# An adaLN block with a Mamba-2 scan: sections in four column groups, the second softplus chain in pieces, and a last stage that projects two tiles ahead

## What is computed

```python
mod = (silu(c) @ wmod).reshape(4, 6, 1, 512)          # sa, ca, ga, sb, cb, gb
ga = sign(ga) * max(|ga|, 0.25); gb likewise
h = layernorm(x) * (1 + ca) + sa
xBCzA = h @ in_proj_w.T                               # 1024 x, 512 B, 512 C, 1024 z, 64 A_log
xBC = silu(conv1d(xBC, 4 taps) + bias)
dt = softplus(A_log)
y = ssd_chunk_scan(x, -dt, B, C) + D * x / dt         # 64 heads of 16, 8 groups, state 64
x = x + ga * ((y * silu(z + z_bias)) @ out_proj_w.T)
h = layernorm(x) * (1 + cb) + sb
x = x + gb * (h @ binarize(w_ffn).T + b_ffn)
```

## Time and profile before

| | |
|---|---|
| median of 3 runs | 722.79 us (719.93 to 724.25) |
| the execution that was profiled | 725.2 us, span in the trace 723.5 us |
| busy, share of the span | PE 91%, DVE 71%, ACT 52%, POOL 52% |
| first stage | to 103.2 us |
| main loop | 103.2 to 583 us |
| last stage | from 583 us |

### The profile page before, as it was taken

How to read it: one execution, slowest core, us unless ns; L and a number is a source line. 1 busy time by engine, 2 the same in 40 slices (tenths; PEclk the granted TensorE clock), 3 DMA queues, 4 the chain that set the end, 5 groups by cost and what they waited for, 6 DMA issues and landing times. The chain is left out here.

```text
span 723.5 us, 21285 instructions
## 1 busy us (share of the span) xinstructions
PE 660.5 (91%) x8347; PEld 497.3 (69%) x8347; DVE 516.7 (71%) x913; ACT 379.1 (52%) x818; POOL 374.9 (52%) x464
## 2 busy tenths in 40 slices
PE   5559797989999999999999999999997999999994
PEld 2244455767777777777777777777775767778783
DVE  3569739796787777777778677777788567676663
ACT  1573633545654545564644564556665545555552
POOL 7544401244653634555445365464556757777771
PEclk9678899999999999999999999999999999999995
DMA  9354211133312121132123143321213755333401
GB/s 265 79 205 121 72 31 54 62 94 106 95 63 93 60 71 65 59 129 67 34 84 104 37 137 107 111 94 49 92 68 101 224 156 153 117 117 117 132 30 43
DMA packets 61915, 70.53 MB, mean 97 GB/s; under 512 B 13972, under 2 KB 33460, under 8 KB 61816
## 3 DMA queue, kind: packets, MB, share of 16 engines
q1 hardware_dynamic: 56376, 69.12, 29.6%
q10 hardware_dynamic: 5440, 0.05, 0.4%
HBM read 54.45 MB, written 14.70 MB: 96 GB/s over the span
## 5 line engine op out<-in xcount | busy, mean ns | idle before, releaser
L1393 DVE SCALAR_TENSOR_TENSOR m_cv<-bank,gpc,m_cv 128x511 f32<-128x511 f32 (+2 forms) x192 | 143.3, 747 | 31.9 <-ACT m_cv L1304 27.3
L1149 PE MATMUL bank<-h_hi,w_hi 128*128 128x512 f32 x384 | 161.0, 419 | 4.8 <-ACT p_hf L647 1.7
L1149 PE MATMUL bank<-h_hi,w_lo 128*128 128x512 f32 x384 | 153.9, 401 | 0.0
L1149 PE MATMUL bank<-h_lo,w_hi 128*128 128x512 f32 x384 | 153.4, 400 | 0.0
L1528 POOL TENSOR_TENSOR m_S<-m_S,m_cd 128x128 f32<-128x128 f32 x96 | 39.7, 413 | 159.3 <-DVE m_S L1453 80.2
L1304 ACT ACTIVATE m_cv<-bank,gpc 128x512 f32<-128x512 f32 x96 | 71.8, 748 | 76.5 <-PE bank L1149 76.5
L1149 PEld LDWEIGHTS bank<-h_hi,w_hi 128*128 128x128 f32 x384 | 74.4, 194 | 20.7 <-issue 6.8
L1149 PEld LDWEIGHTS bank<-h_hi,w_lo 128*128 128x128 f32 x384 | 73.8, 192 | 17.3
L1518 POOL TENSOR_TENSOR m_Xw<-m_Xp,wend 128x256 f32<-128x256 f32 x64 | 39.8, 621 | 87.8 <-ACT m_Xp L1324 87.8
L1149 PEld LDWEIGHTS bank<-h_lo,w_hi 128*128 128x128 f32 x384 | 74.4, 194 | 14.1
L1316 ACT ACTIVATE m_M<-bank 128x512 f32<-128x512 f32 x128 | 76.2, 595 | 12.4 <-PE bank L1158 10.4
(11 more groups left out here) (172 smaller groups left out, 1283.8 us busy)
## 6 DMA issues: line engine op xcount, KB each, us to landing
m_ea<-ea_scratch SPq DMA_DIRECT2D x32, 256.0 KB
m_dd<-dd_scratch SPq DMA_DIRECT2D x32, 256.0 KB
y_scratch<-m_t SPq DMA_DIRECT2D x16, 512.0 KB, 3.3
h_lo_place<-y_scratch SPq DMA_DIRECT2D x16, 512.0 KB, 4.3
p_wm<-in_L_wmod_dram SPq DMA_DIRECT2D x6, 1024.0 KB, 8.1
m_wraw<-in_L_attn_in_proj_w_dram SPq DMA_DIRECT2D x18, 256.0 KB, 3.1
p_xt<-in_L_attn_input__dram SPq DMA_DIRECT2D x16, 256.0 KB, 5.2
w_lo_place<-in_L_attn_input__dram SPq DMA_DIRECT2D x16, 256.0 KB, 4.5
```

The lines of the kernel that those rows point to most:

```text
L1149: ins = pe.matmul(A[k % 3][:, :], w[:, t, kc, :], h[:, n % NB, kc, :], start=(m == 0), stop=(m == 11))
L1393: ins = dve.scalar_tensor_tensor(out=cv[:, k % 3, lag:], in0=A[k % 3][:, 0:L - lag], scalar=s.gpc[:, gp, o:o + 1], in1=cv[:, k % 3, lag:], ...
```

## The change

On PE, `scT` is widened to 32 columns, all but 4 of them zero. `section(n)` now writes product k into partitions 32k to 32k+31 of the bank, with no accumulation, and `turn_section` multiplies the 128 copied rows with `pick`, a 128x4 matrix of ones and zeros, which turns and adds the four parts. The sections 2 to 5 are later in PE's order, and the normalizations 12 to 15 are on POOL. The loads of the sections 0 and 1 come first, x gets eight places instead of four, and the statistics have a place for every tile, which removes waits. `softplus(1)` and `finish_times(1)` are moved from the end of the first stage into the main loop, and `skips(0)` behind the gates:

```diff
             if n == 2:
-                pe.wait_ge(w_act, 8)
-            if n == 4:
-                pe.wait_ge(h_act, 16)
+                pe.wait_ge(h_act, 15)
+                pe.wait_ge(w_act, 12)
+            if n >= 4:
+                pe.wait_ge(sec_cp, n - 1)
             for k in range(KC):
-                ins = pe.matmul(row_bank(n)[0:NB, :], scT[:, k, :], wm[:, n % 2, k, :], start=(k == 0), stop=(k == KC - 1))
+                ins = pe.matmul(row_bank(n)[32 * k:32 * k + 32, :], scT[:, k, :], wm_of(n)[:, k, :], start=True, stop=True)
...
-                ins = pe.transpose(mod_bank(n)[:, k * NB:(k + 1) * NB], row_of(n)[:, k * P:(k + 1) * P], s.ident[0:NB, 0:NB])
+                ins = pe.matmul(mod_bank(n)[:, k * NB:(k + 1) * NB], row_of(n)[:, k * P:(k + 1) * P], pick[:, :], start=True, stop=True)
...
                     if (v, sl) == (-1, 3):
+                        start.softplus(dve, 1)
+                    if (v, sl) == (0, 3):
+                        start.finish_times(dve, 1)
+                    if (v, sl) == (1, 3):
                         start.sums(dve, 1)
-                    if (v, sl) == (1, 3):
+                    if (v, sl) == (2, 3):
                         start.low_sums(dve, 1)
-                    if (v, sl) == (3, 3):
+                    if (v, sl) == (4, 3):
                         start.skips(dve, 1)
```

`store_decays(1)` and `decays(1)` move one unit later with them. DVE and POOL at the start of the first stage, cut:

```diff
 # DVE
         statistics(dve, 0)
-        for i in range(3):
-            statistics(dve, i + 1)
+        statistics(dve, 1)
+        dve.wait_ge(wa_act, 1)
+        dve.tensor_tensor(wa_lo[:, :, 64:128], s.bank[5][:, 0:KC * NH].rearrange("p (k h) -> p k h", k=KC),
+                          wa_hi[:, :, 64:128].bitcast(F32), ALU.subtract).then_inc(wa_dve, 1)
+        for i in range(6):
             normalize(i)
+            if i == 2:
+                modulation(0)
+                modulation(1)
+            statistics(dve, i + 2)
...
+        for i in range(12, 16):
+            statistics(dve, i)
         softplus(dve, 0)
         finish_times(dve, 0)
         sums(dve, 0)
-        skips(dve, 0)
         low_sums(dve, 0)
 # POOL
         constant_fills()
-        for i in range(4):
+        constant_shapes()
+        for i in range(5):
             root(i)
...
+        for i in range(12, 16):
+            normalize(i)
```

In the last stage, project and y are further ahead, POOL keeps one of its three small operations, and the last tile is handled in four pieces:

```diff
 # PE
-            if not is_last(st) and st.n(1, 1) >= 2:
+            if st.n(1, 2) < NB * TT:
                 for part in range(4):
-                    project(pe, st.n(1, 1), part)
+                    project(pe, st.n(1, 2), part)
             turn(st)
             if not is_first(st):
                 linear(st.prev())
 # ACT
         def step(st):
-            normalize(st)
-            if two_more(st):
-                act.wait_ge(ylo_done, st.n(1, 1))
-                high_y(act, st.next().next())
+            if st.n(1, 1) < NB * TT - 1:
+                normalize(st.next())
+            if four_more(st):
+                high_y(act, ahead(st, 4))
...
+            if is_last(st):
+
+                for k in range(KC):
+                    modulated(st, k, h_hi).then_inc(hhi_done, 1)
+                    modulated(st, k, hf).then_inc(hf_done, 1)
+                return
...
+            if is_last(st.next()):
+                normalize(LAST)
 # POOL
-            pool.tensor_tensor(rstd[:, st.b % 2, 0:1], mv[:, st.b % 2, 1:2], eps[:, :], ALU.add).then_inc(eps_done, 1)
...
-            pool.tensor_scalar(rstd[:, st.b % 2, 2:3], mv[:, st.b % 2, 0:1], rstd[:, st.b % 2, 1:2], -1.0,
-                               ALU.mult, ALU.mult).then_inc(rs_done, 1)
-            if two_more(st):
-                low_y(pool, st.next().next())
+            if four_more(st):
+                low_y(pool, ahead(st, 4))
 # DVE
+        dve.tensor_scalar(rstd[:, st.b % 2, 0:1], mv[:, st.b % 2, 1:2], EPS, None, ALU.add).then_inc(eps_done, 1)
+        dve.tensor_scalar(down[:, st.b % 2:st.b % 2 + 1], mv[:, st.b % 2, 0:1], -1.0, None, ALU.mult).then_inc(eps_done, 1)
```

More of the change, by code:

```diff
@@ L422, in gpsimd @@
             weights(n)
-        root(10)
-        root(11)
+        for i in range(8, 16):
+            root(i)
+        weights(4)
+        weights(5)
+        for i in range(12, 16):
+            normalize(i)
+        weights(6)
+        weights(7)
+        pool.wait_ge(a_v[0], A_END)
         low_part(8)
         low_part(10)
-        for n in range(4, 8):
-            weights(n)
-        for i in range(12, 16):
-            root(i)
         low_part(12)
@@ L538, in vector @@
         low_part(13)
+        convolve(2)
         low_part(15)
-        convolve(2)
         silu(1)
@@ L547, in vector @@
         gates()
[L548 to L549 removed]
+        skips(dve, 0)
     def chained(dve, pb, count):
@@ L687, in scalar @@
         softplus_inputs(0)
+        make_h(8)
+        make_h(9)
+        weights(4)
+        weights(5)
+        make_h(10)
+        make_h(11)
+        linear(0)
+        weights(6)
+        weights(7)
+        linear(1)
+        decays(act, 0)
+        linear(2)
+        tanh(0)
+        make_h(12)
+        make_h(13)
+        tanh(1)
+        make_h(14)
+        make_h(15)
         for n in range(8, 12):
-            make_h(n)
-        for n in range(4, 8):
             weights(n)
-        linear(0)
-        decays(act, 0)
         copy_row(2)
         copy_row(3)
-        linear(1)
-        for n in range(12, 16):
-            make_h(n)
-        linear(2)
-        tanh(0)
-        for n in range(8, 12):
-            weights(n)
-        tanh(1)
         linear(3)
@@ L794, in weights @@
             ins.then_inc(wt_pe, 1)
-        pe.wait_ge(sct_ready, 1)
+        pe.wait_ge(cond_step, 4)
+        section(0)
+        section(1)
         pe.wait_ge(d_wa, 16)
         for k in range(KC):
-            ins = pe.transpose(DTB[:, k * NH:(k + 1) * NH], wa_raw[:, k * P:(k + 1) * P], s.ident[0:NH, 0:NH])
+            ins = pe.transpose(s.bank[5][:, k * NH:(k + 1) * NH], wa_raw[:, k * P:(k + 1) * P], s.ident[0:NH, 0:NH])
         ins.then_inc(wa_pe, 1)
-        turn(0)
-        turn(1)
-        section(0)
-        turn(2)
-        turn(3)
-        section(1)
+        pe.wait_ge(sec_cp, 2)
         turn_section(0)
         turn_section(1)
-        for i in range(4, 8):
+        for i in range(8):
             turn(i)
@@ L812, in tensor @@
             weights(n)
-        pe.wait_ge(wa_dve, 1)
         dt_inputs(0)
-        pe.wait_ge(w_act, 4)
         for i in range(8, 12):
             turn(i)
-        for n in range(4, 8):
-            weights(n)
+        weights(4)
+        weights(5)
         project(0, 0)
         project(0, 1)
+        project(1, 0)
+        project(1, 1)
+        weights(6)
+        weights(7)
+        project(2, 0)
+        project(2, 1)
+        for i in range(12, 16):
+            turn(i)
+        for n in range(8, 12):
+            weights(n)
         section(2)
         section(3)
-        project(1, 0)
-        project(1, 1)
+        project(3, 0)
+        project(3, 1)
         turn_section(2)
         turn_section(3)
-        for i in range(12, 16):
-            turn(i)
-        project(2, 0)
-        project(2, 1)
-        for n in range(8, 12):
-            weights(n)
-        project(3, 0)
-        project(3, 1)
         section(4)
         section(5)
-        pe.wait_ge(w_act, 12)
         end_turn(pe, 0)
+        pe.wait_ge(h_act, 16)
+        dt_inputs(1)
         turn_section(4)
         turn_section(5)
-        dt_inputs(1)
         pe.wait_ge(gate_v, 3)
@@ L1682, in step @@
                 main.store_last(sp)
-            else:
-                store(st.prev())
+            if two_back(st):
+                store(ahead(st, -2))
         run(step)
+        store(ahead(LAST, -1))
         store(LAST)
@@ L1717, in step @@
                 act.wait_ge(main.t1_done, 2 * STEPS)
+            wait(act, hlo_done, st.n(1, -1))
+            if is_last(st):
+                for k in range(KC):
+                    modulated(st, k, h_hi).then_inc(hhi_done, 1)
+                    modulated(st, k, hf).then_inc(hf_done, 1)
+                return
             for k in range(KC):
[L1719 to L1720 removed]
+                ins = modulated(st, k, h_hi)
             ins.then_inc(hhi_done, 1)
[L1722 removed]
             for k in range(KC):
[L1725 to L1726 removed]
+                ins = modulated(st, k, hf)
             ins.then_inc(hf_done, 1)
+            if is_last(st.next()):
+                normalize(LAST)
+        high_y(act, ahead(FIRST, 2))
+        normalize(FIRST)
+        high_y(act, ahead(FIRST, 3))
         run(step)
```

295 lines of the change are left out of this document (159 added, 136 removed).

## The result

The changed kernel takes **716.55 us** (median of 8 runs, 714.72 to 717.99), the kernel before 724.39 on the same chip (8 runs, 719.93 to 725.7). The ratio is 0.9903, 95% interval 0.9877 to 0.9929: faster by about 1%, 7.0 us by the ratio and 7.8 by the medians. Of 23 executions of the kernel before in the first group of experiments, fifteen took 720.1 to 724.0 us and eight took 725.1 to 726.7, so a median of few executions depends on the mix. I had forecast 706.7 and a range of 700.5 to 714.0. So the sign is right, the gain is somewhat less than half of the 16.1 us forecast, and the result lies outside the range. The profiled execution took 717.52 us, with a span of 715.5, which is 8.0 less than the 723.5 of before; the forecast was 16.1 less.

A forecast was written before the change was run, and what follows sets the result against it. PE was taken to bound the kernel, busy 660.5 of 723.5 us, with idle time mainly in the first and last stages. 722.8 - 3 (first stage) - 13.1 (last stage) = 706.7 us; range 700.5 to 714.

The forecast's parts named there:

- rival 5: Last stage: its 5.9 us aren't gained, ACT's wait for project(n+2) replacing its wait for POOL; 712.6 us, chance 0.09.
- rival 1: End of the last stage: the clock falls in the last gap, 3.4 us more, 710.1 us; chance 0.23.
- rival 2: First stage: the sections don't overlap, sections 2 to 5 cost 14.1 instead of 5.2 us; 715.6 us, chance 0.07.
- the row on the diagonal: Main-loop diagonal product: 3.4 us of columns done in 0.86, fourfold overlap; basis for 0.9 us a section.
- rival 6: First stage: POOL's normalizations hold up the first chain, stretching its other half by 2.7 us; 709.4 us, chance 0.06.
- the sum for the first stage: First stage into main loop: loop begins at 98.9, not 103.24; 4.3 us shrink to about -3, bounds -8 and +1.
- The walk through DVE: Main loop: following DVE's order with present durations, m_Ct's second-batch silu ends at 130.8 instead of 134.4.
- rival 4: Turns -1 to 4: chain pieces stop PE and halve its clock; 17 us lost cancel the gain, 25 give 731; chance 0.03.
- Rival 3: Main loop: pieces go under DVE's slack, PE gains 4.3 + 4.6 instead of 3 us; 701 us, chance 0.12.
- The gain of the last stage: Last stage: -5.9 from waits inside, -0.2 at the start, -4.7 and -2.3 at the end; -13.1 us.
- its bound for the first stage, +1: First stage: upper bound of the -3 us sum, if each chain piece stops PE once.

The follow-up runs named there:

- e4: The change with each section again four accumulated 4-row matmuls, turned by 4-row transposes, in the new order; 725.53 us, ratio 1.0024 to the kernel before.
- e5: The change with normalizations 12 to 15 back on DVE behind the first chain; 716.60 us, ratio 0.9922 to the kernel before.
- e2: The change with the last stage of the kernel before, so the new first stage alone; 726.76 us, ratio 1.0053 to the kernel before.
- e6: The change with x tiles 0 to 3 normalized and turned before the section rows are turned; 713.49 us, ratio 0.9878 to the kernel before.
- e3: The change with the second softplus chain in one piece and the first reciprocal back in their old places; 716.96 us, ratio 0.9910 to the kernel before.
- e11: The kernel before with the new last stage, turns 13 and 14 inside the last projection, and the first reciprocal moved into DVE's idle time; 710.90 us, ratio 0.9824.
- e10: The change with x turned first, second chain begun behind the gates, first reciprocal in DVE's idle time, turns 13 and 14 inside the last projection; 711.01 us, ratio 0.9827.
- e9: The change itself measured once more, nothing altered, against the kernel before; 716.47 us, ratio 0.9905.
- e7: The change with the first reciprocal in DVE's idle time after 83 and the second chain begun right behind the gates; 715.63 us, ratio 0.9902.

## Why the prediction was wrong, and where it was right

**Right.** PE alone bounds the last stage, and the period is 7.90 us (rival 5 falls). The clock stays at full speed across the last gaps of 1.43 and 0.97 us (rival 1 falls; it wasn't tried what a gap of 2.3 in one piece does, so that this came out right is in part luck: the gap was split by a wait that I hadn't foreseen). The sections overlap, at 0.96 us each (1.92 for the pair 4 and 5) against 3.60 in e4, where I had 0.9 (rival 2 falls). The estimate from the Trainium skill (TensorE: Matmul & The Clock Gate, Measured speedup vs the span model) was 1.1 to 1.5 us; the measurement decides for the row on the diagonal. POOL's normalizations hold up the chain by less than 1 us and the loop not at all (rival 6 falls, by e5), though each takes two to four times what I gave it. The rule of the Trainium skill (SBUF — State Buffer, Who interferes with whom) agrees with the trace in direction, 0.89 us a step beside POOL's work against 0.72 without; for the chain it changes nothing here, since POOL has other work in that time in either kernel. It costs something behind the chain, where I had not looked for it: the 2.88 us for DVE's two subtractions.

**The step that failed: the sum for the first stage, "-3".** The trace has +1.6 at project 2 (+1.0 at the ninth product), and e2 has +4.3 us on the whole. Nearly all of it was there when the loop began: at 98.9 in the forecast and at 104.14 in the trace, 5.2 us later. My own points of time show where it came from:

- *The start, 2.7 us.* h of tile row 0 begins at 28.18, not at 26. I had looked at which loads and which DVE work stood ahead of the first h, and had left out PE's own order: the turns of the section rows, 3.57 us, and behind them the transposes of x, which in the kernel before were done while ACT was issuing loads. At the end of the first dt_inputs it is 2.9 us (50.95, not 48.0), at the beginning of the chain 3.2 (54.75, not 51.6), and at the end of its sums 2.7 are left. e6 undoes just this and gets 2.5 us back.
- *Between the sums and the last weights on ACT, 2.0 us.* ACT is done with w_act 12 at 84.4, not 79.8, so 4.6 late. ACT waits for the convolution, which stands behind DVE's two subtractions for h_lo, and these take 2.88 us beside POOL's two instead of 1.28, which is 1.6 of the 2.0. No run tests this term by itself.
- *The turns by `pick`, 2.4 us.* I had 0.6 for a pair, it takes 1.84, and two pairs stand behind 84. I priced it by the old turn, eight for eight, and didn't ask what had changed in one: a matmul of fp32 has two records where the old transpose has one (x16 and x8 in the rows), and one record takes 0.115 us where that of 4 rows took 0.083.
- *The other way, 1.9 us.* Project 3 takes 2.9 us, not 3.5, and ACT's three inputs to the second chain run beside the last turns, so that 1.8 us lie between these and the loop and not 3.1. (2.7, 2.0 and 2.4 less 1.9 make the 5.2.)

In the last step I let DVE's end of one silu stand for PE. It ended 2.8 us later than before, while PE's ninth diagonal product of the loop came 1.0 us later (181.25 and 182.29). The walk through DVE was good to 1 us once its start is put right (it begins 5.4 late and ends 6.4 late). But one number at 131 isn't the cost of many short waits. PE did get what the stall had cost: its first diagonal product stands at 117.99, 3.9 us earlier than before. It lost this again to the pieces: the second product is 0.4 us later than before (129.39 and 128.97), the fourth 2.4 (145.69 and 143.33). In that stretch lie waits of 2.64, 1.08, 0.65 and 0.49 us, and a half clock behind the first of them (0.94 over 104 to 160, 0.83 from 120 to 130). That is rival 4's mechanism, far from its size. Rival 3 is refuted: by e3, the pieces and the moved reciprocal together gain at most 1.4 us in this place, not the 4.6 of the stall and the 4.3 before it.

**The gain of the last stage was over-sized by 3 us.** From project 2 to the end I had 121.7 us, measured are 124.6 (134.2 before). 1.7 lie inside: 1.13 of it is linear 0 waiting for h_lo, in a period that I had taken for a regular one though it is the first in which DVE's `split` is wanted. 1.2 lie behind the last projection, 16.5 instead of 15.3. The idle time there is 2.4 us as forecast, in two gaps and not in one, but linear 14 and 15 take 4.5 us, not 4.1, and the rest behind them 4.3, not 3.9. And of the 0.6 us by which project 2 was to begin earlier 0.2 came: its wait for y_lo is 1.33 where it was 1.53.

With the first stage at its measured +1.6 and the last at -9.6 the sum gives -8.0, the difference of the two spans. The range was too narrow on its upper side: its bound for the first stage, +1, assumed every start up to the loop as known, although the order of three engines had been rewritten there.

## What to carry to other kernels

A faster instruction is worth what the place costs into which it is put: here the sections became nearly four times faster and were moved onto the path with a dearer turn behind them, so that the old order with one reciprocal moved into idle time (e11) did better than the change and as well as the change with three repairs (e10). When the start of a stage is reordered, follow every engine's order to the first product that all else hangs on, the bottleneck engine's included; of a start 3.4 us earlier, 2.5 were left 75 us later. And long work on a shared engine, such as a reciprocal of 3.8 us, belongs in a gap that the trace shows, before one cuts up the rest.

## What was not expected of the hardware

- A matmul of four moving columns isn't cheap: eight in fp32 with 128x128 stationary take 1.84 us behind 90 us, 0.23 each in two records, against 0.08 for a transpose of 4 rows in one record (0.66 for eight). PE's weight loads (PEld) are busy 1.75 of the 1.77 us from 90.82 on.
- The granted clock that a trace shows need not fit the lengths of its rows near the start: that of the change reads 1.00 up to 69 us, yet the eight turns at 20.99 take 3.57 us, twice as long as behind 90. So the mean granted clocks of the two kernels (0.979 for the change, 0.963 before) don't compare.
- POOL needs 2.65 us for subtract and multiply on 128x512 (10.58 for four, beside DVE's chain), where DVE needs 0.55. Its subtraction of one such tile from another takes 1.27.
- In the change the granted clock was 0.83 from 120 to 130 us, with a PE gap of 2.64 us in it, while a single gap of 4.6 us before 117 had left it at full speed while it lasted. And after the same two gaps ahead of the loop, 1.1 and 0.36 us, the clock was at half for 3.4 us (105 to 108.8) in the change, at half there too in e2, e5 and e9, and stayed full in e6, e7 and e10.
- The main loop from the ninth product to its end took 406.1 to 409.4 us in fourteen traces, the new last stage 124.6 in eight. Whole executions of the kernel before on one chip took 720.1 to 726.7.
